# Mixture of experts in 64-row tiles, image by image, with the shared experts one chunk ahead

## The reference

```python
shared = zeros_like(h)
for s in range(2):                      # 2 shared experts
    shared = shared + gelu(c1(feats, shared_w[s], shared_b[s])) / 2
vals, idx = top_k(scores, 4)
wts = softmax(vals / 2.0, axis=1)       # per image
gate_w = zeros((B, 16)).at[arange(B)[:, None], idx].add(wts)
out = shared
for e in range(16):
    out = out + gelu(c1(feats, expert_w[e], expert_b[e])) * gate_w[:, e][:, None, None, None]
return out + residual
```

## Time and profile before

| | us |
|---|---|
| median of 3 runs | 7425.35 (7419.53 to 7432.88) |
| profiled execution, its own time | 7437.15 |
| its span | 7435.4 |
| PE busy / DVE / ACT / POOL | 6438.8 / 5528.0 / 3983.0 / 3926.6 |
| stage `experts`, first load issued to last store issued | 2643.87 to 3019.82 |
| of it, DVE's weight building to the first matmul | 2653.29 to 2684.19 |

### The profile page before, as it was taken

One profiled execution on the slowest core, in us unless ns is written; L12 is line 12 of the kernel. 1 busy time (PEld: TensorE's weight loads), 2 busy tenths in 40 slices (PEclk: granted clock), 3 DMA queues, 4 the chain that ended last, 5 costly groups with the idle time before them and its releaser, 6 DMA issues. The chain is left out here.

```text
span 7435.4 us, 119549 instructions
## 1 busy us (share of the span) xinstructions
PE 6438.8 (87%) x36560; PEld 3391.8 (46%) x36560; DVE 5528.0 (74%) x5048; ACT 3983.0 (54%) x6942; POOL 3926.6 (53%) x2716
## 2 busy tenths in 40 slices
PE   8968699999987369776999999999899999999970
PEld 7852233333355124565222222222267777777750
DVE  4653577777722268211999999999989999999975
ACT  4425466666621457201767677676555555555532
POOL 0100122222200300000999999999889999999960
PEclk9989799999988689856999999999989999999985
DMA  2253233334345623434222222222100000000026
GB/s 71 71 168 133 64 99 100 100 96 100 100 127 120 262 82 102 132 91 65 39 41 38 41 37 41 38 40 39 26 16 10 10 10 9 10 9 10 9 43 191
DMA packets 638162, 518.33 MB, mean 70 GB/s; under 512 B 249981, under 2 KB 569251, under 8 KB 629563
## 3 DMA queue, kind: packets, MB, share of 16 engines
q1 hardware_dynamic: 637947, 515.62, 28.3%
HBM read 304.91 MB, written 171.32 MB: 64 GB/s over the span
## 5 line engine op out<-in xcount | busy, mean ns | idle before, releaser
L2311 POOL TENSOR_TENSOR spa_hc<-spa_hs,spa_cr 128x966 f32<-128x966 f32 x592 | 1314.1, 2240 | 41.6 <-DVE spa_hs L2605 38.7
L2605 DVE TENSOR_TENSOR_SCAN spa_hs<-spa_p_d,spa_hs,spa_bx 128x967 f32<-128x967 f32 x584 | 1304.3, 2233 | 0.7 <-ACT spa_p_d L2504 0.7
L2749 POOL TENSOR_TENSOR spe_hc<-spe_hs,spe_bcu 128x1024 f32<-128x1024 f32 x520 | 1219.7, 2362 | 65.5 <-DVE spe_hs L2961 64.7
L2961 DVE TENSOR_TENSOR_SCAN spe_hs<-spe_p_d,spe_bx 128x1024 f32<-128x1024 f32 x520 | 1161.1, 2274 | 36.4 <-ACT spe_p_d L2909 33.0
L2836 PEld LDWEIGHTS spe_p_y<-spe_idt,spe_hc 128*128 128x128 f32 x8320 | 966.4, 192 | 143.5 <-issue 143.5
L1065 DVE TENSOR_REDUCE attention_nm<-attention_p_s 128x2 f32<-128x640 f32 x1024 | 788.6, 811 | 261.3 <-PE attention_p_s L922 260.1
L2836 PE MATMUL spe_p_y<-spe_idt,spe_hc 128*128 128x128 f32 x8320 | 979.7, 276 | 0.0
L1023 ACT ACTIVATE attention_pr<-attention_p_t 128x512 f32<-128x512 f32 x1280 | 710.7, 599 | 426.0 <-PE attention_p_t L945 289.7
L2504 ACT ACTIVATE spa_p_d<-spa_p_d,spa_av 128x483 f32<-128x483 f32 x1184 | 704.0, 634 | 376.5 <-PE spa_p_d L2375 376.5
L2909 ACT ACTIVATE spe_p_d<-spe_p_d 128x896 f32<-128x896 f32 x520 | 445.5, 900 | 760.2 <-PE spe_p_d L2819 759.9
L2375 PE MATMUL spa_p_d<-spa_du,spa_hot 32*128 32x483 f32 x2368 | 644.4, 619 | 12.6 <-DVE spa_hs L2605 3.2
(11 more groups left out here) (427 smaller groups left out, 10621.6 us busy)
## 6 DMA issues: line engine op xcount, KB each, us to landing
attention_qs<-scratch_qp SPq DMA_DIRECT2D x768, 64.0 KB, 2.8
spa_uc<-spa_du SPq DMA_DIRECT2D x148, 241.5 KB
attention_rc<-scratch_den SPq DMA_DIRECT2D x128, 256.0 KB
scratch_qp<-patch_parts SPq DMA_DIRECT2D x64, 384.0 KB, 2.3
spa_xt<-scratch_x SPq DMA_DIRECT2D x148, 121.5 KB, 2.7
front_xs<-in_x_dram SPq DMA_DIRECT2D x64, 256.0 KB, 2.9
scratch_xf<-front_out SPq DMA_DIRECT2D x128, 128.0 KB, 2.5
patch_x<-scratch_xf SPq DMA_DIRECT2D x8, 2048.0 KB, 18.7
```

What stands on the lines that cost most here:

```text
L2311: nc.gpsimd.tensor_tensor(hc[:, k % 8:k % 8 + 2, :], hs[:, k:k + 2, 0:NA], cr2[:, s % 2, :].unsqueeze(1).broadcast_to([128, 2, NA]), ALU.m ...
L2605: last = nc.vector.tensor_tensor_scan(joined(hs, j), p_d[j % 2][:, 511 - NA:512 + NA], joined(bx, j), hs[:, k, NA - 1:NA], ALU.mult, ALU.add)
L2749: nc.gpsimd.tensor_tensor(hc[:, k, :, d, :].rearrange("p s d t -> p d s t"), hs[:, k % 2, d, :, :], rows, ALU.mult)\
L2961: nc.vector.tensor_tensor_scan(hs[:, k % 2, d].rearrange("p d s t -> p (d s t)"), p_d[h][:, :], bx[:, k % 2, d].rearrange("p d s t -> p (d ...
```

## The change

Only the stage `experts`, the layout of the shared experts' weights on the host, and the place of the helpers `after` and `stream` in the file are changed.

- Matmuls. Instead of one 128x128 block matrix per expert for two images, each matmul takes the 64 partitions of one image and two experts side by side (64 rows, 128 columns): `spread_shared` gives both shared experts, `spread(0)` the first two chosen ones, `spread(2)` the last two, each for image p = 0 and p = 1 into a bank of its own (`p_x[k][p]`). Six matmuls a chunk as before, now of 64 rows. A result has one expert in partitions 0 to 63 and another in 64 to 127.
- `add_halves`: for each image a matmul of 128 rows and 64 columns with `fold` (two stacked identities) adds the two halves into its half of `p_o`. Two more matmuls a chunk.
- ACT: six gelus a chunk as before, the two of the shared experts now written to SBUF (`gs`).
- POOL: scales the shared experts by 1/2 (`scale`, two products of 128x512 a chunk, into `us`).
- DVE: `add_first` (two adds: gate times chosen pair plus `us`), `add_last` (two adds), `finish` (`p_o` plus `hr`). Five instructions a chunk instead of six.
- Order: the loop is written with `stream`, which unrolls four chunks and gives each part a lag. The shared experts run one chunk ahead of the chosen ones; fold and `finish` run one chunk behind. Consecutive chunks alternate between the two pairs of images (a = s % 2).
- Buffers: `fs` four deep, loads issued up to three chunks ahead; stores lag five steps.
- Setup: the chosen experts' weights lie side by side, so that one sum covers all 128 partitions (8 sums in place of 16); every second product with the one-hot row runs on POOL. 13 DMAs instead of 14, of which four gather every second expert's gate or one-hot row (`hot2`, `gx`).

```diff
@@ experts: PE
+            def spread_shared(c, s, r):
+                pe.wait_ge(f_in[s], 16 * r + 16)
+                for p in range(2):
+                    after(pe, shared_active, 2 * c + (p - 1))
+                    rows = slice(64 * p, 64 * p + 64)
+                    nc.tensor.matmul(p_x[1][p][:, :], wsh[rows, :], fs[rows, s, :], start=True, stop=True).then_inc(shared_done, 1)
+            def spread(k, free):
+                def run(c, s, r):
+                    for p in range(2):
+                        after(pe, free, 2 * c + (p - 1))
+                        rows = slice(64 * p, 64 * p + 64)
+                        nc.tensor.matmul(p_x[k][p][:, :], wx[rows, s % 2, k // 2, :], fs[rows, s, :], start=True, stop=True).then_inc(x_done, 1)
+                return run
+            def add_halves(c, s, r):
+                after(pe, out_ready, c - 1)
+                for p in range(2):
+                    pe.wait_ge(last_added, 2 * c + (p + 1))
+                    mm = nc.tensor.matmul(p_o[s % 2][64 * p:64 * p + 64, :], fold[:, :], acc[:, s % 2, p, :], start=True, stop=True)
+                mm.then_inc(folded, 1)
+            stream(pe, NCH, UX, UX, 2, (1, spread(0, first_added)), (0, spread_shared), (1, spread(2, last_added)), (2, add_halves))
-                        for k in range(NX):
-                            pe.wait_ge(summed[k], n)
-                            mm = nc.tensor.matmul(p_x[k][:, :], wx[:, a, k, :], fs[:, s, :], start=True, stop=True)
-                            mm.then_inc(x_done, 1)
@@ experts: ACT
+            stream(act, NCH, UX, UX, 1, (1, activate(0, first_active)), (0, activate_shared), (1, activate(2, last_active)))
@@ experts: DVE, setup
+            def choose(a, k, t):
+                nc.vector.tensor_reduce(wx[:, a, k // 2, C * (k % 2):C * (k % 2) + C], pk[:, t], AX.X, ALU.add).then_inc(w_ready, 1)
-                    for q in range(2):
-                        r = slice(64 * q, 64 * q + 64)
-                        last = nc.vector.tensor_reduce(wx[r, a, NSH + k, 64 * q:64 * q + 64], pk[r], AX.X, ALU.add)
-                        link(last)
@@ experts: DVE, loop
+            def add_first(c, s, r):
...
+                    dve.wait_ge(first_active, 2 * c + (p + 1))
+                    dve.wait_ge(shared_scaled, 2 * c + (p + 1))
+                    after(dve, folded, c - 1)
+                    nc.vector.scalar_tensor_tensor(acc[:, t, p, :], p_x[0][p][:, :], gx[:, b(p), 0:1], us[:, t, p, :], ALU.mult,
+                                                   ALU.add).then_inc(first_added, 1)
+            def add_last(c, s, r):
...
+                    dve.wait_ge(last_active, 2 * c + (p + 1))
+                    dve.wait_ge(first_added, 2 * c + (p + 1))
+                    nc.vector.scalar_tensor_tensor(acc[:, t, p, :], p_x[2][p][:, :], gx[:, b(p), 1:2], acc[:, t, p, :], ALU.mult,
+                                                   ALU.add).then_inc(last_added, 1)
+            def finish(c, s, r):
+                dve.wait_ge(folded, c + 1)
+                after(dve, stored[s % 2], 16 * (r * 2 + s // 2))
+                nc.vector.tensor_tensor(os[:, s % 2, :], p_o[s % 2][:, :], hr[:, s % 2, columns(s, r)], ALU.add).then_inc(out_ready, 1)
+            stream(dve, NCH, UX, UX, 2, (1, add_first), (2, finish), (1, add_last))
@@ experts: POOL
+            def scale(c, s, r):
+                for p in range(2):
+                    pool.wait_ge(shared_active, 2 * c + (p + 1))
+                    after(pool, first_added, 2 * c + (p - 3))
+                    nc.gpsimd.tensor_tensor(us[:, s % 2, p, :], gs[:, s % 2, p, :], share[:, :], ALU.mult).then_inc(shared_scaled, 1)
+                nc.gpsimd.tensor_tensor(pk[:, 1], wes[:, :, :], hot[:, a, k, :].unsqueeze(1).broadcast_to([128, C, NE]), ALU.mult)\
+                    .then_inc(halved, 1)
+            stream(pool, NCH, UX, UX, 0, (0, scale))
@@ experts: SP
+            def load(c, s, r):
+                after(sp, x_done, 4 * (c - 3))
+                sp.dma_start(fs[:, s, :], feats[:, s % 2, columns(s, r)]).then_inc(f_in[s], 16)
+            stream(sp, NCH, UX, 2 * UX, 5, (0, load), (5, store))
```

More of the change, by code:

```diff
@@ L66, in turns, with after, stream, fixed @@
     return run
+def after(eng, sem, n):
+    if not (isinstance(n, int) and n <= 0):
+        eng.wait_ge(sem, n)
+def stream(eng, n, unroll, head, tail, *parts):
+    def fixed(i):
+        for lag, part in parts:
+            c = i - lag
+            if 0 <= c < n:
+                part(c, c % unroll, c // unroll)
+    for i in range(head):
+        fixed(i)
+    with eng.Fori(0, (n - head) // unroll - 1) as j:
+        for s in range(unroll):
+            for lag, part in parts:
+                c = head + s - lag
+                part(j * unroll + c, c % unroll, j + c // unroll)
+    for i in range(n - unroll, n + tail):
+        fixed(i)
 KH = H // 2
@@ new lines, in experts @@
+        gx = st.sb("gx", [128, B, TOP // 2])
+        idt = st.sb("idt", [128, 128])
+        fold = st.sb("fold", [128, C])
+        share = st.sb("share", [128, 512])
+        fs = st.sb("fs", [128, UX, 512])
+        gs = st.sb("gs", [128, 2, 2, 512])
+        us = st.sb("us", [128, 2, 2, 512])
+        acc = st.sb("acc", [128, 2, 2, 512])
+        os = st.sb("os", [128, 2, 512])
+        p_x = [[st.ps(f"p_x{k}{p}", [128, 512]) for p in range(2)] for k in range(NP)]
+        p_o = [st.ps(f"p_o{s}", [128, 512]) for s in range(2)]
@@ L1868, in _ @@
[L1868 to L1871, removed]
+                    b = 2 * a + p
+                    sp.dma_start(hot[64 * p:64 * p + 64, a].rearrange("p k e -> p (k e)"),
+                                 sel.rearrange("b k e -> b (k e)")[b:b + 1, :].broadcast_to([64, TOP * NE])).then_inc(loaded, 16)
+            with nc.allow_non_contiguous_dma(reason="every other expert's gate"):
+                for q in range(2):
+                    r = slice(64 * q, 64 * q + 64)
+                    sp.dma_start(hot2[r], sel.rearrange("b (k q) e -> q (b k) e", q=2)[q:q + 1].broadcast_to([64, B * TOP // 2, NE]))\
+                        .then_inc(loaded, 16)
+                    sp.dma_start(gx[r].rearrange("p b k -> p (b k)"),
+                                 wts.rearrange("b (k q) -> q (b k)", q=2)[q:q + 1].broadcast_to([64, B * TOP // 2])).then_inc(loaded, 16)
@@ L1885, in _, with activate_shared @@
[L1885 to L1894, removed]
[L1896 to L1898 removed]
+            def activate_shared(c, s, r):
+                for p in range(2):
+                    act.wait_ge(shared_done, 2 * c + (p + 1))
+                    after(act, shared_scaled, 2 * c + (p - 3))
+                    nc.scalar.activation(gs[:, s % 2, p, :], p_x[1][p][:, :], ACT.Gelu, bias=bsh[:, 0:1]).then_inc(shared_active, 1)
@@ new lines, in activate, with run @@
+            def activate(k, active):
+                def run(c, s, r):
+                    for p in range(2):
+                        b = 2 * (s % 2) + p
+                        act.wait_ge(x_done, 4 * c + (k + p + 1))
+                        nc.scalar.activation(p_x[k][p][:, :], p_x[k][p][:, :], ACT.Gelu, bias=bx[:, b, k // 2:k // 2 + 1]).then_inc(active, 1)
+                return run
+            act.wait_ge(w_ready, 2 * TOP + 2)
+            stream(act, NCH, UX, UX, 1, (1, activate(0, first_active)), (0, activate_shared), (1, activate(2, last_active)))
@@ L2081 @@
 TD = TK * DE
-def after(eng, sem, n):
-    if not (isinstance(n, int) and n <= 0):
-        eng.wait_ge(sem, n)
 RA = 7
```

152 lines of the change are left out of this document (57 added, 95 removed).

## The result

Median of six runs each: 7417.75 us before (7412.60 to 7432.88), 7466.88 us after (7453.15 to 7473.10). The ratio is 1.0061, 95% interval 1.0051 to 1.0071. I had forecast 7360, in a range of 7335 to 7395.

A forecast was written before the change was run, and what follows sets the result against it. PE was taken to bound the experts' loop at 5.15 us a chunk, DVE's chain 0.2 behind. Loop -52 and setup -13 gave -65 us, so a median of 7360 us, range 7335 to 7395.

The forecast's parts named there:

- The rest of the program has the same instructions: All stages outside the experts: no change expected; anything over 3 us there would count against the forecast.
- Loads, +2: Experts' setup: short-piece gate and one-hot loads cost 2 us more, bounds -0.5 to +6.
- My own sign of being wrong: Experts' setup: DVE's first product later than 2657 would show the forecast wrong.
- DVE's setup, 15.9: Building the experts' weights on DVE: 15.9 us for 30.9, a gain of 15.0.
- Just hidden: Experts' setup: POOL's 2.36 us product fits behind DVE's product and sum (2.5); if late, 4 x 0.3 at most.
- Setup in all: Experts' setup, DVE's work and loads together: 13 us less.
- The loop, 4.3 a chunk, 284 us: Experts' loop of 64 chunks: 4.3 us each, bounds 4.1 to 4.6, plus 9 for start and end; 284 for 335.6.
- The round: Experts' loop: second add last, last-expert matmul, fold, finish, first add last form a closed path of 4.26 us a chunk.
- rival 2: Experts' loop on PE: 64-row matmul pairs do not overlap, 7.2 us a chunk, 7546 us; chance 0.07 together with rival 3.
- a change of form: Experts' loop on PE: switching matmul tiling mode, twice a chunk, costs 0.14 to 0.20 us each, taken as 0.17.
- rival 3: Experts' loop: PE's clock drops; at 1.2 GHz a chunk takes 7.2 us or more; chance 0.07 together with rival 2.
- rival 1: Experts' loop: ACT draining PSUM binds at 3.97 us a chunk, not the round; 7339 us; chance 0.12.

The follow-up runs named there:

- a_pe64: The changed kernel with 64 more instructions of long-fulfilled waits on PE, moving its spectral loop from 25878 to 25942: 7384.97 us, ratio to before 0.9943.
- b_pe207: The kernel before with 207 more wait instructions ahead of PE's experts loop, so its spectral loop starts at 25878 as in the changed kernel: 7519.19 us, ratio 1.0134.
- a_loads: The changed kernel plus 64 PE waits, with gates and one-hots loaded as whole rows and every other expert picked on DVE: 7360.50 us in one run.
- a_best: The changed kernel plus 64 PE waits, DVE's finish last, whole-row loads, three product buffers, POOL's first product held until DVE's first is done: 7333.93 us, ratio 0.9880.
- a_order: The changed kernel plus 64 PE waits, with DVE's finish behind the two add_last instead of ahead of them: 7337.14 us, ratio 0.9882.

## Why the prediction was wrong, step by step

- **The step that failed**: "The rest of the program has the same instructions; anything over 3 us there would also go against me." It has the same instructions at other positions, and a loop of 100 KB now stands where its code is fetched anew in each of 12 turns, for 7.6 us a turn. I put this term at nothing and gave no reason beyond the unchanged instructions; none of the rivals named it. In place of 0 it measured +91.5, shown from both sides (a_pe64, b_pe207).
- **Loads, +2**: measured +9.8, above my upper bound of +6. I went by the issue time of the row nearest and bounded the landing by a guess; the issue is 0.64 for 0.60, the landing is what grew (a_loads). My own sign of being wrong, DVE's first product later than 2657 or 13.1 us after the first load, came true: 22.0 (2657.14 - 2635.12).
- **DVE's setup, 15.9**: measured 20.3. "Just hidden" took POOL's 2.36 from a group and let it run beside DVE's products. The bias product lost 2.1 us (2.43, where in a_best one of the same length over 64 partitions takes 0.28) and each of three turns 0.83 (4.59 from 2660.65 to 2665.24, for 3.76), where I had bounded the whole by 4 x 0.3. Setup in all: -0.8 us for my -13.
- **The loop, 4.3 a chunk, 284 us**: 4.40 and 288.6, inside the bounds. The round was right. The step that I had too short is the fold until DVE reads it, which I had at 1.18 and which takes 1.24 and 1.34 in two chunks (2804.76 to 2806.00, 2809.11 to 2810.45).
- **Pairs overlap** (rival 2): right, 0.86 to 0.96 for my 0.86; the steps at a change of form 0.09 and 0.15 longer (0.95 and 1.01 less 0.86 in a_order) for 0.17, but the step from first to shared experts, with no such change, is 0.10 longer too, so the price of a change alone is not shown. **Clock** (rival 3): 1.00 in the loop (2700 to 2950). **PSUM emptying** (rival 1): did not bind, even in a_order.
- With the place put right, a_pe64 stands at 7384.97, 25 us over the forecast: 7.8 from the loads, 4.4 from DVE's setup, 4.6 from the loop, and 8 that are within the spread. That it lies inside my range (7335 to 7395) is in part luck: the range was made for the loop, and of the 13 us that the setup should bring it brought 0.8.

## What to carry to other kernels

Where a kernel has a long hardware loop on PE (here 100 KB of code), an edit ahead of it moves the loop's code: look for the instruction queue's packets inside the loop and for "issue" gaps of one per turn, and if they are there, move the loop before judging the edit (here 32 and 64 instructions were enough). Count a load of short pieces by its landing, not by its issue. A product on two SBUF inputs that is moved to POOL is not free beside DVE products of that kind: release it when DVE's product is done, so that it runs beside the sums. And in a software pipeline, put the consumer that waits for another engine's last step behind the ones that feed that engine: this one swap was worth 34 us in the stage (287.5 to 254 from first matmul to last store), for the 47.5 of the whole change.

## What I had not expected of the hardware

- Two loads of 512 pieces of 4 bytes take 6.6 and 12.5 us to land; the whole row, 16 values to each of 128 partitions, takes 3.7 (a_loads).
